# Columns of a transformed convolution ordered by output half: strided reads in TensorE's matmuls, and joins on VectorE straight from PSUM

## The reference

```python
qkv = conv1x1(batchnorm(x), qkv_w, qkv_b).reshape(B, 3, HEADS, HD, H, W)       # B=4, HEADS=6, HD=32
qk = concatenate([q * scale, k], axis=1)                                       # 64 channels per head
attn = conv(qk, dm_w, 7x7, pad 3) + dm_b                                       # 49 outputs per pixel
attn = softmax(attn + rel_bias, axis=taps)
out = einsum('bnckhw,bnkhw->bnchw', patches(v, 7x7), attn)                     # weighted sum of 49 neighbours
```

## Time and profile before

| | |
|---|---|
| median of 3 runs | 6478.28 us (6477.91 to 6493.02) |
| the profiled execution | 6477.91 us, with a span of 6476.3 us |
| instructions | 88803 |
| TensorE (PE) busy | 86% of the span |
| VectorE (DVE) busy | 70% |
| ScalarE (ACT) busy | 43% |
| GpSimd (POOL) busy | 13% |
| the changed stage's loop over slots | about 380 us to 1880 us of the span |

### The profile page before, as it was taken

The page is one execution under the profiler, slowest core; times in us unless marked ns, Lnnn a source line. Parts: engine busy times, 40 slices in busy tenths (PEclk is TensorE's granted clock), DMA queues, the critical chain, the costliest instruction groups (busy, mean ns, idle before and its releaser), DMA issues. The chain is left out here.

```text
span 6476.3 us, 88803 instructions
## 1 busy us (share of the span) xinstructions
PE 5542.9 (86%) x34700; PEld 2540.7 (39%) x34700; DVE 4507.7 (70%) x5404; ACT 2786.0 (43%) x3983; POOL 813.2 (13%) x868
## 2 busy tenths in 40 slices
PE   6959999999969978978877999968858898888877
PEld 2435455455434433445533344423313333333323
DVE  3267777777721112278976567769979999999978
ACT  1213333333322212335522544425548777777733
POOL 0000000000000001122242000000113333333300
PEclk9989999999979989999988999978979999999989
DMA  6431121121121114344433000012220000000035
GB/s 150 124 66 21 36 39 21 36 39 21 18 62 66 67 39 151 114 138 137 140 124 107 9 26 28 24 42 67 74 62 16 26 20 19 25 26 6 15 96 154
DMA packets 314735, 397.18 MB, mean 61 GB/s; under 512 B 159804, under 2 KB 296260, under 8 KB 311084
## 3 DMA queue, kind: packets, MB, share of 16 engines
q1 hardware_dynamic: 297580, 313.73, 18.0%
q0 software_dynamic: 16768, 78.09, 3.5%
HBM read 225.25 MB, written 166.50 MB: 60 GB/s over the span
## 5 line engine op out<-in xcount | busy, mean ns | idle before, releaser
L3573 DVE TENSOR_TENSOR_SCAN s_h<-s_da,s_h 128x448 f32<-128x448 f32 x672 | 728.9, 1122 | 1.1 <-ACT s_da L3500 1.0
L3420 PE MATMUL s_py<-s_prod,s_idf 128*128 128x448 f32 x1344 | 587.7, 560 | 23.8 <-ACT s_ycol L3513 22.6
L504 PE MATMUL b_pc<-b_ca,b_wdm 128*113 128x392 f32 x1152 | 485.8, 518 | 57.1 <-DVE b_idb L877 55.7
L3500 ACT ACTIVATE s_da<-s_dt,s_al 128x448 f32<-128x448 f32 x672 | 405.7, 657 | 199.0 <-DVE s_h L3573 148.8
L636 ACT ACTIVATE b_band<-b_psel 124x784 f32<-124x784 f32 x192 | 158.3, 824 | 602.4 <-PE b_psel L561 602.3
L504 PE MATMUL b_pc<-b_cb,b_wdm 128*113 128x392 f32 x960 | 407.8, 525 | 0.0
L3558 DVE TENSOR_TENSOR s_h<-s_dtu,s_pb 128x896 f32<-128x896 f32 x336 | 354.2, 1054 | 30.0 <-POOL s_dtu L3607 23.5
L929 DVE TENSOR_SCALAR b_band<-b_psel 124x784 f32<-124x784 f32 x192 | 186.7, 973 | 263.4 <-PE b_psel L561 261.1
L3580 DVE TENSOR_TENSOR s_prod<-s_h,s_pc 128x896 f32<-128x896 f32 x336 | 360.0, 1071 | 0.1
L3420 PEld LDWEIGHTS s_py<-s_prod,s_idf 128*128 128x128 f32 x1344 | 249.7, 193 | 219.9 <-issue 167.9
L3596 POOL TENSOR_TENSOR s_dt<-s_dt,s_dtu 128x448 f32<-128x448 f32 x168 | 249.2, 1483 | 507.2 <-DVE s_h L3573 425.5
(11 more groups left out here) (565 smaller groups left out, 11543.3 us busy)
## 6 DMA issues: line engine op xcount, KB each, us to landing
mid_qkvp<-a_out SPq DMA_DIRECT2D x84, 372.0 KB, 4.0
b_qk<-mid_qkvp SPq DMA_DIRECT2D x96, 240.2 KB
d_vt<-mid_vd SPq DMA_DIRECT2D x200, 96.0 KB
d_qs<-mid_qd SPq DMA_DIRECT2D x20, 744.0 KB, 5.0
d_ks<-mid_kd SPq DMA_DIRECT2D x20, 744.0 KB, 7.6
b_v<-mid_qkvp SPq DMA_DIRECT2D x6, 1922.0 KB
mid_pout<-d_out POOLq DMA_DIRECT2D x20, 558.0 KB, 4.4
mid_x1p<-c_out POOLq DMA_DIRECT2D x14, 744.0 KB, 4.0
```

Source lines behind the costliest of these rows:

```text
L504: mm = pe.matmul(pc[n % 2][0:113, 0:392], wdm[:, slot, p, 0:113], src, start=(w == STARTS[a]), stop=(w + 1 == STARTS[a + 1]))
L3420: mm = pe.matmul(y, idf[:, :], prod[j % 3][:, e, :], start=(pr == 0 and e == 0), stop=False)
L3500: last = a.activation(da[j % 4][:, e, :], dt[s % 2][:, span(c)], ACT.Exp, scale=al[:, u, n:n + 1])
L3573: v.tensor_tensor_scan(x, along(da[j % 4][:, e, :]), x, before_, ALU.mult, ALU.add).then_inc(scanned, 1)
```

## The change

The 392 columns of each convolution matmul are now read in the order row, half, tile pair: `src` is read as 28 rows by 2 halves by 7 elements that lie two elements (8 bytes) apart, where it was read as 28 rows of 14 elements side by side. The PSUM results come in that order, and `column` and `sevens` view `lg` and the operands as 56 runs of 7 elements. `copy_shares` and its semaphore are gone; `inner` reads result 4 from PSUM itself, in four operations with the factors -0.5, 0.25, 1 and -0.125. The first matmul of group 6 waits for `inner` in place of `copy_shares`, and `pair2` waits for `joined` in place of `inner_ready`.

```diff
                     if a == 6:
-                        pe.wait_ge(shares_copied, 2 * (h + 1))
+                        pe.wait_ge(inner_ready, 4 * (h + 1))
...
-                mm = pe.matmul(pc[n % 2][0:113, 0:392], wdm[:, slot, p, 0:113], src, start=(w == STARTS[a]),
-                               stop=(w + 1 == STARTS[a + 1]))
+                mm = pe.matmul(pc[n % 2][0:113, 0:392], wdm[:, slot, p, 0:113], src.rearrange("p h (i c) -> p h c i", c=2),
+                               start=(w == STARTS[a]), stop=(w + 1 == STARTS[a + 1]))
...
-            def copy_shares(h):
-
-                a.wait_ge(conv_done, 7 * h + 5)
-                a.wait_ge(joined, 4 * (h + 1))
-                a.activation(p2[:, :], pc[7 * h % 2][0:113, 0:392], ACT.Copy, scale=-0.5).then_inc(shares_copied, 1)
-                a.activation(m2[:, :], pc[7 * h % 2][0:113, 0:392], ACT.Copy, scale=0.25).then_inc(shares_copied, 1)
-
...
-                if h is not None and r == 36:
-                    copy_shares(h)
...
-            fours = lambda t: t.rearrange("p (h i t) -> p h i t", i=NI, t=2)
-            column = lambda h, e: lg[0:113, :, :].rearrange("p h (t e i) -> p e h i t", t=2, e=4)[:, e, :, :, :]
+            sevens = lambda t: t.rearrange("p (a i) -> p a i", i=NI)
+            column = lambda h, e: lg[0:113, :, :].rearrange("p h (t e i) -> p (h t) e i", t=2, e=4)[:, :, e, :]
...
                 if h:
-                    v.wait_ge(inner_ready, 4 * h)
+                    v.wait_ge(joined, 4 * h)
                 v.tensor_tensor(p2[:, :], two[:, :], got(h, 3), ALU.add).then_inc(pair2_ready, 1)
...
             def inner(h):
 
+                v.wait_ge(conv_done, 7 * h + 5)
                 v.wait_ge(joined, 4 * (h + 1))
                 if h:
                     v.wait_ge(turned, 4 * h)
-                v.wait_ge(shares_copied, 2 * (h + 1))
-                v.scalar_tensor_tensor(one[:, :], p2[:, :], -2.0, one[:, :], ALU.mult, ALU.add).then_inc(inner_ready, 1)
-                v.scalar_tensor_tensor(m1[:, :], p2[:, :], 0.25, m1[:, :], ALU.mult, ALU.add).then_inc(inner_ready, 1)
-                v.tensor_tensor(column(h, 1), fours(p2[:, :]), fours(two[:, :]), ALU.add).then_inc(inner_ready, 1)
-                v.tensor_tensor(column(h, 2), fours(m2[:, :]), fours(p1[:, :]), ALU.add).then_inc(inner_ready, 1)
+                v.scalar_tensor_tensor(column(h, 1), sevens(got(h, 4)), -0.5, sevens(two[:, :]), ALU.mult, ALU.add).then_inc(inner_ready, 1)
+                v.scalar_tensor_tensor(column(h, 2), sevens(got(h, 4)), 0.25, sevens(p1[:, :]), ALU.mult, ALU.add).then_inc(inner_ready, 1)
+                v.tensor_tensor(one[:, :], got(h, 4), one[:, :], ALU.add).then_inc(inner_ready, 1)
+                v.scalar_tensor_tensor(m1[:, :], got(h, 4), -0.125, m1[:, :], ALU.mult, ALU.add).then_inc(inner_ready, 1)
...
-                v.tensor_tensor(column(h, 0), fours(got(h, 5)), fours(one[:, :]), ALU.add).then_inc(first_ready, 1)
+                v.tensor_tensor(column(h, 0), sevens(got(h, 5)), sevens(one[:, :]), ALU.add).then_inc(first_ready, 1)
...
-                v.tensor_tensor(column(h, 3), fours(got(h, 6)), fours(m1[:, :]), ALU.add).then_inc(last_ready, 1)
+                v.tensor_tensor(column(h, 3), sevens(got(h, 6)), sevens(m1[:, :]), ALU.add).then_inc(last_ready, 1)
```

More of the change, by code:

```diff
@@ L366, in window_attention @@
         two_copied = sem("b_two_copied")
-        shares_copied = sem("b_shares_copied")
         pair1_ready = sem("b_pair1_ready")
```

## The result

The changed kernel took 6525.28 us (median of 4 runs, 6520.77 to 6528.06), the kernel before 6479.8 us over all its runs beside it. The ratio is 1.0065, with a 95% interval of 1.0047 to 1.0083: 0.65% slower, where 0.37% less had been forecast, and above the upper end of the range of 6504. The profiled execution took 6517.37 us for a span of 6515.7.

A forecast was written before the change was run, and what follows sets the result against it. TensorE, busy 1274 of 1333 us, was taken to set the pace, so other engines' savings count only where it waits. 7.8 + 5.3 + 2.0 + 8.6 = 23.7 us off 6478.3 gave 6454.6 us, range 6448 to 6504.

The forecast's parts named there:

- I take 0: TensorE's convolution matmuls, 2496 passes of 329 ns: reading elements 8 bytes apart was claimed to add nothing.
- The row of POOL: POOL adding elements 8 bytes apart: 2.31 ns an output against 2.23 side by side, taken to show a free step.
- The other far row: VectorE at a 16-byte step: 0.79 ns an element more; on all TensorE elements 308 ns a pass, +769 us.
- The second rival: TensorE's read pays for 42 lone elements a pass: 33 ns a pass, +83 us, 6537 us; chance 0.20.
- `first` and `last`, 7.8 us: VectorE joins writing runs of 7 shorten 16 TensorE waits at psel by 0.49 us each, from 1.87 to 1.38.
- The third rival: VectorE's runs of 7 write as slowly as alternating places: 6.3 us gained, 6472 us; chance 0.09.
- `copy_shares`, 5.3 us: Removing ScalarE's copies ends a hidden 0.18 us TensorE wait at r=36 in 22 heads and 1.32 us in the second.
- The first head, 2.0 us: Only there TensorE waits for inner's chain, 5.34 us for L868; of this 2.0 us come back.
- The clock, 8.6 us: Six lowered-clock stretches behind the 1.87 us psel waits, 8.7 us in all, end with waits of 1.38 us.
- the first rival: TensorE's clock is lowered as often as before: 15.1 us gained, 6463 us; chance 0.27, wholly or partly.
- `inner`, worth nothing: VectorE's inner gains 1.5 us, which only lengthens idle time ahead of first from 0.5 to about 2.0, 22 times.
- no drops of the clock behind the shorter waits of the stage: TensorE's lowered-clock stretches were found only behind six of the 16 waits of 1.87 us at psel.

The follow-up runs named there:

- read_only: The kernel before with only TensorE's strided read of the convolution's moving operand added; 6537.85 us, ratio 1.0097.
- joins_only: The changed kernel with TensorE's moving operand read side by side again, values landing in wrong columns; 6453.35 us, ratio 0.996.
- psum_order: The changed kernel with columns read side by side and the reordering made by TensorE's write into PSUM; 6455.67 us, ratio 0.9966.
- shares_only: The kernel before without the two ScalarE copies, inner adding result 4 from PSUM, alternating writes kept; 6482.05 us, ratio 1.0006.
- writes_only: The kernel before with ScalarE copies kept, TensorE writing PSUM in the new order and joins writing runs of 7; 6460.23 us, ratio 0.9969.
- steps_before: The kernel before with VectorE's steps of the next head issued at r=45, ahead of first, instead of r=47; 6460.38 us, ratio 0.9973.
- steps_early: psum_order with VectorE's steps of the next head issued at r=45, ahead of first, instead of r=47; 6430.59 us, ratio 0.9928.

## Why the prediction was wrong

**What failed is one step: "I take 0, since the step is that of the POOL row and since TensorE asks for an element only every 0.84 ns."** The strided read costs 45 ns a pass (374 against 329 ns). A pass is on the path, 2496 times: 112 us. In `read_only` 112 - 64 = 48 of these came back from TensorE's shorter waits and from the clock, and the rest showed. The row of POOL that it leaned on was that of another engine, which takes 2.2 to 2.3 ns for an output; a read that keeps up with that says little of one element in 0.84. The other far row, VectorE's 0.79 ns for an element alone in 16 bytes, was the near one: the runs gave TensorE 0.6 to 1.0 for a lone element and 0.9 for a step of 16 bytes.

**The second rival was right in kind.** It gave 33 ns a pass for 42 lone elements at 0.79 ns. Measured are 29 ns for 28 to 30 of them, at 1.0 ns: two errors that nearly cancel. The 17 ns more for the step itself it had not. It named 9.5 ns as the point of decision, and 45 is past that. The Trainium skill's rule (two accesses in a row in one 16-byte line go at full bandwidth; "SBUF — State Buffer", the note on cachelines in "Door 1: The DMA port swizzle") agrees with the traces in what it says of lone elements. By it long runs of step 2 would be free, and they are nearly so: 346 against 329 ns.

**The rival's sum was too high because a slower TensorE absorbs its own waits.** It gave 6537 us with 33 ns a pass; with 45 ns it would have given 6478.3 + 112 - 23.7 = 6567. `read_only` shows why that is too much. In a head of its steady part, 104 passes of 44 ns (536 - 492) are 4.6 us more; the distance of two waits grew only by 62.33 - 59.46 = 2.9 (1048.59 to 1110.92). The wait at `psel` gave back 1.02 us of it, the two for `pr` 0.44 (0.71 and 0.28 us became one of 0.55), the one hidden at r=36 up to 0.18; under 0.1 us is not assigned. Over the stage the 16 waits at `psel` gave back 16.3 us, those for `pr` 8.7 (23.5 to 14.8), the clock 8.7 and r=36 up to 4.0; some 10 of the 48 us are not assigned. That the rival's 6537 us lies near the measured 6525 is luck: its price was too low by 12 ns a pass, and it gave nothing back. What TensorE waited for ahead of its matmuls into `ptr` (us, times), by the answer for that tile, in the kernel before:

```profile
  DVE b_pr L894: 23.5, 46
```

and in `read_only`:

```profile
  DVE b_pr L894: 14.8, 24
```

**What the joins and the ScalarE copies bring was forecast rightly.** The sum was 23.7 us; `joins_only` has 22.9 less in the stage and `psum_order` 26.6. Term by term:

- *`first` and `last`, 7.8 us.* The wait became 1.42 us where 1.38 was forecast, 16 x 0.45 = 7.2. The third rival, runs of 7 as slow as alternating places, is out: 0.56 us.
- *`copy_shares`, 5.3 us.* `shares_only` shows the 0.17 in each head, and in the stage 4.0, or about 6 without the two further drops of the clock.
- *The first head, 2.0 us.* In `joins_only` the wait for L858 is 4.94 us, only 0.40 less, but a second one of 1.36 us that the prediction hadn't seen (group 6 for `first`, 1.36 us in the trace of before) has gone too: 1.8 us.
- *The clock, 8.6 us.* In `joins_only`, `psum_order`, `writes_only` and `steps_before`, with waits of 1.4 us, no stretch of lowered clock followed any of the 16; in `shares_only`, with 1.87 us, eight did. So the first rival is out. The trace of after has none there either, its mean from 474 to 1850 us is 1.00.
- *`inner`, worth nothing.* True as the work stood: the idle time ahead of `first` grew to 1.82 us in `joins_only` and to 2.52 in the kernel after. `steps_early` shows what it was good for: the same move of `steps` takes 16 x 1.42 = 22.7 us off the waits, where it takes 7.7 off with 0.5 us of idle time.

The prediction is wrong where it found no drops of the clock behind the shorter waits of the stage. At its end, where no convolution is left beside the last selections, the kernel before waits at `psel` for VectorE (1.14 us) and ScalarE (0.98 us) in turn, one wait every 1.6 to 1.7 us. TensorE is busy for 29 of the 50 us in the window below, and the clock, the third number from the right, is 0.73 there in the mean and 0.50 from 1848 to 1864 us:

```profile
1851.28 0.59 PE L561 MATMUL b_psel<-b_at,b_sel 64*124 64x196 bf16 x4 [1.14 <-DVE b_band L929]
...
1854.58 0.58 PE L561 MATMUL b_psel<-b_at,b_sel 64*124 64x196 bf16 x4 [1.15 <-DVE b_band L929]
...
1830.00:1880.00 50.00, 29.21 (x470) 21.04 (x468) 10.69 (x11) 19.16 (x33) 0.00 (x0) 0.73 0.06 14
```

All nine kernels that were timed here do this at the stage's end. So the length of a single wait doesn't decide by itself.

The second wait of the first head in the timeline of TensorE in the kernel before:

```profile
419.03 2.86 PE L504 MATMUL b_pc<-b_ca,b_wdm 128*113 128x392 f32 x8 [1.36 <-DVE b_lg L862]
```

In the kernel after, the joins save less than in `joins_only`: 64.2 - 48.0 = 16.2 us. Of these 16 x (0.85 - 0.37) = 7.7 are the `psel` waits, as much as in `joins_only` (7.2); the 8.7 us of the clock are missing, since the slower read had ended the drops already.

## What to carry to other kernels

Price the access pattern of the operand that the bound engine reads before anything else: here a free-looking step of two elements cost 14% of each pass on the engine that was busy 96% of the stage, while the gain lay on an engine with spare time. Where a layout has to be changed by somebody, try the write into PSUM before the read: the same order cost nothing there. And when an engine off the path gets idle time ahead of a critical stretch, move work out of that stretch into it; the idle time by itself brings nothing.

## What the runs showed of the hardware

- An fp32 matmul pass of 392 columns takes 329 ns read side by side, 346 with a step of 8 bytes in long runs, 375 in runs of 7, and 683 to 700, twice as long, when each element lies alone in its 16 bytes. An element alone in its 16 bytes cost 0.6 to 1.0 ns more.
- TensorE writing fp32 columns alternately to places 28 bytes apart in PSUM took the same 329 ns.
- VectorE writing 392 fp32 elements to alternating places took 0.87 to 0.89 us, and 0.56 us when the same elements went out in runs of 7.
- In the heads with all work interleaved, short stretches of TensorE's clock at half its level came behind waits of 1.87 us in six of 16 cases of the kernel before and eight of 16 of `shares_only`, and behind none of 64 waits of about 1.4 us in four kernels. At the end of the stage, with waits of 0.98 to 1.15 us one every 1.6 to 1.7 us, the clock was at half its level too (0.50 from 1848 to 1864 us in the kernel before).
